# One pipeline of 24 chunks for the third feed-forward, with x in three bf16 parts, and a reordered first stage

## What is computed

```python
x = x + tanh(g_xattn[0]) * L0_xattn(ctx, norm(x))     # similarity graph, top 76 of each row
x = x + tanh(g_ffn[0])   * L0_ffn(norm(x))            # mixture of 16 experts, 6 chosen, and a shared one
x = x + tanh(g_xattn[1]) * L1_xattn(norm(x), ctx)     # latent attention, 16 heads
x = x + tanh(g_ffn[1])   * L1_ffn(norm(x))            # the one called "ternary" below
x = x + tanh(g_xattn[2]) * L2_xattn(norm(x), ctx, ctx)
x = x + tanh(g_ffn[2])   * L2_ffn(norm(x))
x = x + tanh(g_xattn[3]) * L3_xattn(norm(x), ctx)
x = x + tanh(g_ffn[3])   * L3_ffn(norm(x))

def quantize(w):                       # L1_ffn: weights become -1, 0 or 1
    return clip(round(w / (mean(abs(w)) + 1e-8)), -1, 1)
def L1_ffn(x, w1, w2, w3):             # w1, w2: 704 x 256, w3: 256 x 704
    x1, x2 = x @ quantize(w1).T, x @ quantize(w2).T
    return (sigmoid(x1) * x2) @ quantize(w3).T
```

## Time and profile before

| | us |
|---|---|
| median of 3 runs | 875.55 (875.4 to 877.6) |
| the profiled execution | 877.72, of it a span of 875.6 |

### The profile page before, as it was taken

One profiled execution on the slowest core, in us unless ns is written; L12 is line 12 of the kernel. 1 busy time (PEld: TensorE's weight loads), 2 busy tenths in 40 slices (PEclk: granted clock), 3 DMA queues, 4 the chain that ended last, 5 costly groups with the idle time before them and its releaser, 6 DMA issues.

```text
span 875.6 us, 13499 instructions
## 1 busy us (share of the span) xinstructions
PE 808.7 (92%) x4982; PEld 622.1 (71%) x4982; DVE 507.1 (58%) x1189; ACT 355.4 (41%) x1172; POOL 139.6 (16%) x146
## 2 busy tenths in 40 slices
PE   6799999999999999899997899998999999999973
PEld 3688888888888887677675567885667666666742
DVE  4677657657765534455567642325777664674742
ACT  2211111111111111667664661115887775675730
POOL 0000120000000000000019700001343233232001
PEclk9999999999999999999999999997999999999985
DMA  8970200000011002300000000000000000000000
GB/s 281 375 174 3 82 1 1 1 1 1 1 60 40 0 1 80 104 1 1 1 1 1 1 1 1 1 0 0 2 1 2 1 1 1 1 2 13 5 23 12
DMA packets 16175, 28.02 MB, mean 32 GB/s; under 512 B 3648, under 2 KB 11824, under 8 KB 15856
## 3 DMA queue, kind: packets, MB, share of 16 engines
q1 hardware_dynamic: 16112, 27.19, 9.7%
HBM read 26.13 MB, written 1.05 MB: 31 GB/s over the span
## 4 chain that ended last, share of the span: by engine, by line
PE 80%; DVE 8%; ACT 7%; issue 2%; POOL 1%; DMA 0%; SPq 0%; ACTq 0%; DVEq 0%; POOLq 0%
PE PS L1478 20%; PE PS L1502 10%; PE PS L1707 5%; PE PS L1731 5%; PE PS L1682 5%; PE PS L1567 3%; PE PS L1757 3%; ACT arena L734 3%; PE PS L1672 3%; ACT arena L816 2%; PE PS L1583 2%; DVE arena L1150 2%; PE PS L1611 2%; PE PS L1599 2%; PE PS L1626 2%
## 5 line engine op out<-in xcount | busy, mean ns | idle before, releaser
L656 ACT ACTIVATE arena<-PS 128x256 f32<-128x256 f32 (+3 forms) x192 | 102.1, 559 | 97.9 <-PE PS L1567 39.1
L816 ACT ACTIVATE arena<-PS,W_d 128x256 f32<-128x256 f32 (+1 forms) x256 | 110.6, 449 | 8.7 <-DVE W_d L1216 4.4
L524 POOL TENSOR_TENSOR RS<-MV,eps 128x2 f32<-128x2 f32 x32 | 6.2, 195 | 652.9 <-DVE MV L932 635.8
L1478 PE MATMUL PS<-XT,W_g 128*128 128x256 f32 (+1 forms) x400 | 98.0, 388 | 0.0
L1478 PE MATMUL PS<-XT,W_u 128*128 128x256 f32 (+1 forms) x400 | 95.2, 380 | 0.0
L1502 PE MATMUL PS<-W_d,mlp_tmp 128*128 128x256 f32 (+1 forms) x400 | 94.1, 379 | 0.0
L698 ACT ACTIVATE tanh_g<-PS 128x512 f32<-128x512 f32 x48 | 28.7, 597 | 156.7 <-PE PS L1478 156.7
L1093 DVE TENSOR_TENSOR mlp_tmp<-mlp_tmp,PS 128x512 f32<-128x512 f32 (+1 forms) x52 | 34.7, 667 | 86.3 <-PE PS L1489 86.1
L1478 PEld LDWEIGHTS PS<-XT,W_u 128*128 128x128 f32 (+1 forms) x400 | 76.0, 190 | 11.0
L1478 PEld LDWEIGHTS PS<-XT,W_g 128*128 128x128 f32 (+1 forms) x400 | 74.6, 192 | 10.9 <-issue 1.2
L1502 PEld LDWEIGHTS PS<-W_d,mlp_tmp 128*128 128x128 f32 (+1 forms) x400 | 72.2, 190 | 8.7
(11 more groups left out here) (209 smaller groups left out, 1376.2 us busy)
## 6 DMA issues: line engine op xcount, KB each, us to landing
W_d<-in_w_d SPq DMA_DIRECT2D x1, 3072.0 KB, 10.6
arena<-in_wq SPq DMA_DIRECT2D x4, 512.0 KB, 6.1
arena<-in_wo1T SPq DMA_DIRECT2D x4, 512.0 KB, 7.8
W_g<-in_w_g SPq DMA_DIRECT2D x2, 1024.0 KB, 9.4
W_u<-in_w_u SPq DMA_DIRECT2D x2, 1024.0 KB, 11.3
arena<-in_wkq1T SPq DMA_DIRECT2D x4, 384.0 KB, 6.8
mlp_w<-in_w SPq DMA_DIRECT2D x1, 1408.0 KB, 6.0
W_g<-in_w_g SPq DMA_DIRECT2D x1, 1120.0 KB, 12.2
```

What stands on the lines that cost most here:

```text
L656: last = act.activation(dst, src, ACT.Copy)
L816: last = act.activation(PL[:, n % 2, k * S:k * S + w], PS[:, bank + x, i * S:i * S + w], ACT.Exp, bias=NML[:, n % 2, k:k + 1], accum_out=D ...
L1478: last = mm(PS[0:m, k, e * S:(e + 1) * S], w[:, d, f0:f0 + m], XT[p][:, d, :], start=d == 0, stop=d == 1)
```

## The change

It has seven parts.

1. Ternary becomes one list of 24 chunks g = 6b + k across the batches. PE runs `up1(g)` and `down1(g - 2)`; chunks rotate through banks 2, 3 and 4, the sum through 5 and 6. The transposes of the next x come at k = 2.
2. The signs of w1 and w2 are written in bf16 (`w12b`), and the normalised x is split into three bf16 parts (`XB`) whose sum is x: ACT copies the high part out of PSUM (`high_part`), POOL makes the other two (`parts_of`: subtract, copy, subtract, 512 columns each). `up1` is then 12 bf16 products in place of 4 in fp32. w3 and the hidden rows stay in fp32.
3. `up1(0)` and `up1(1)` stand among the last latent items; `late_scores(0)` stands ahead of `up1(23)`, `late_scores(1)` ahead of `down1(23)`. ACT writes the first queries straight from PSUM, and `late_exponents(0)` stands ahead of the tanh of chunk 23.
4. First stage: projections of one batch each instead of two; the similarity of batch 0 is formed after the first of them. All four steps of fold 0 stand ahead of `graph_turn(0)`, `fold(1, 0)` behind it and `fold(1, 3)` behind the first `turn`. The ten steps left run in batch 0 of the experts, two for each pass c = 3 to 7. On DVE the graph's `graph_norm(0)` moves from behind the mask to between rounds 2 and 3. SP issues fold group 1 earlier, and slices 1 and 2 of the expert weights behind waits for fold steps.
5. Latent start: `stats(1)` and the first normalisation move from between the first items into passes 11 and 12 of the experts' last batch; the first keys use bank 7 instead of 6.
6. Late: PE's `job_turn` moves from ahead of `late_turned` to the end of the item; ACT's `job_turned` moves behind its `late_turned`, and its `job_mixed` ahead of `late_exponents`.
7. Two additions of a bias and one normalisation at the start of late move from DVE to POOL.

```diff
+def ternary_fills():
+    order = []
+    for g in range(CHUNKS):
+        order.append((2 + g % 3, "up", g // CH1, g % CH1))
+        if g >= 2 and (g - 2) % CH1 == 0:
+            b = (g - 2) // CH1
+            order += [(5 + b % 2, "y", b, 0), (7, "turn", b, 0)]
+    return order
...
+START_FOLDS = [(0, 0), (0, 1), (0, 2), (0, 3), (1, 0), (1, 3)]
+LATER_FOLDS = [(1, 1), (1, 2), (2, 0), (2, 3), (2, 1), (2, 2), (3, 0), (3, 3), (3, 1), (3, 2)]
...
@@ gpsimd
-                pool.tensor_tensor(wf, wf, less[0:parts, 0:n], ALU.subtract).then_inc(ternary_ready, 1)
+                signs = w12b[:, 2 * k:2 * k + 2, :].rearrange("p a b -> p (a b)") if k < 2 else wf
+                pool.tensor_tensor(signs, wf, less[0:parts, 0:n], ALU.subtract).then_inc(ternary_ready, 1)
...
+            def parts_of(b):
+
+                bank, value = fill_at("ternary", "turn", b - 1) if b else fill_at("latent", "turn", NB - 1)
+                pool.wait_ge(drained[bank], value)
+                x, (high, mid, low) = XT[b % 2][:, :, :].rearrange("p c s -> p (c s)"), [XB[b % 2][:, k, :] for k in range(3)]
+                pool.tensor_tensor(rest, x, high, ALU.subtract).then_inc(part_split, 1)
+                pool.wait_ge(part_split, 2 * b + 1)
+                pool.tensor_copy(mid, rest).then_inc(part_split, 1)
+                pool.wait_ge(part_split, 2 * b + 2)
+                pool.tensor_tensor(low, rest, mid, ALU.subtract).then_inc(parts_ready, 1)
+                pool.wait_ge(parts_ready, b + 1)
+
+            parts_of(0)
+            for b in range(NB):
+                rstd(next_no("ternary", b))
+                if b + 1 < NB:
+                    parts_of(b + 1)
...
@@ scalar
+            def high_part(b, bank, value):
+
+                act.wait_ge(filled[bank], value)
+                act.activation(XB[b % 2][:, 0, :], PS[:, bank, :], ACT.Copy)
...
+            for g in range(1, CHUNKS):
+                b, k = g // CH1, g % CH1
+                hidden_tanh(g)
+                if k == 2 and b + 1 < NB:
+                    bank, value = fill_at("ternary", "turn", b)
+                    high_part(b + 1, bank, value)
+                    xt_out(value, (b + 1) % 2, bank)
+                elif k == 2:
+                    first_queries()
+                if g == CHUNKS - 2:
+                    late_exponents(0)
...
@@ scalar, late
-                if p == 5 and r:
-                    job_turned(r)
                 if p == 7 and r:
                     job_exp(r)
                 if n < ITEMS:
                     late_turned(n)
+                if p == 1 and r > 1:
+                    job_mixed(r - 1)
+                if p == 5 and r:
+                    job_turned(r)
...
@@ vector
+            for g in range(CHUNKS):
+                b, k = g // CH1, g % CH1
+                hidden_rows(g)
+                if k == 0:
+                    stats((b + 1) % NB)
+                if k == 1:
+                    ternary_next(b)
+                    if b:
+                        output("ternary", b - 1, CA[:, 2:3])
+                    else:
+                        output("latent", NB - 1, TG[:, 1:2])
...
+                if g == CHUNKS - 2:
+                    late_maximum(0)
             late_maximum(1)
+            output("ternary", NB - 1, CA[:, 2:3])
...
@@ tensor
+            def up1(g):
...
+                if k == 0:
+                    pe.wait_ge(parts_ready, b + 1)
+                bank = begin("ternary", "up", b, k)
+                for w in range(2):
+                    for c in range(2):
+                        for part in range(3):
+                            last = mm(PS[0:m, bank, w * S:(w + 1) * S], w12b[:, 2 * w + c, k * P:k * P + m],
+                                      XB[b % 2][:, part, c * S:(c + 1) * S], start=c == 0 and part == 0,
+                                      stop=c == 1 and part == 2)
+                last.then_inc(filled[bank], 1)
...
+            for b in range(2):
+                projected(b)
+                similarity(b)
+            projected(2)
+            fold(0, 0)
+            similarity(2)
+            projected(3)
+            fold(0, 1)
+            similarity(3)
+            fold(0, 2)
+            fold(0, 3)
+            pe.wait_ge(first_loaded, 16 * N_FIRST)
             graph_turn(0)
-            fold(0, 3)
+            fold(1, 0)
             turn(1, fill_at("moe", "turn", -1)[1] - 1)
+            fold(1, 3)
...
+            for g in range(2, CHUNKS):
+                b, k = g // CH1, g % CH1
+                if g == CHUNKS - 1:
+                    late_scores(0)
+                    down1(g - 3)
+                up1(g)
+                if g < CHUNKS - 2:
+                    down1(g - 2)
+                if k == 2:
+                    turn(next_no("ternary", b), fill_at("ternary", "turn", b)[1] - 1)
+            down1(CHUNKS - 3)
+            down1(CHUNKS - 2)
+            late_second_banks = fill_at("ternary", "up", NB - 1, CH1 - 2)
+            pe.wait_ge(drained[late_second_banks[0]], late_second_banks[1])
             late_scores(1)
+            down1(CHUNKS - 1)
```

More of the change, by code:

```diff
@@ L95, in biases_before @@
 def biases_before(what, r):
-    order = []
+    order = [("late", 0), ("late", 1)]
     for n in range(ROUNDS + 1):
@@ L184, in late_fills, with later_folds, fold_phase, graph_phase @@
     return order
+START_FOLDS = [(0, 0), (0, 1), (0, 2), (0, 3), (1, 0), (1, 3)]
+LATER_FOLDS = [(1, 1), (1, 2), (2, 0), (2, 3), (2, 1), (2, 2), (3, 0), (3, 3), (3, 1), (3, 2)]
+def later_folds(c):
+    m = 2 * (c - FOLD_AT)
+    return LATER_FOLDS[m:m + 2] if m >= 0 else []
+def fold_phase(n, k):
+    return "begin" if (n, k) in START_FOLDS else "moe"
+def graph_phase(b):
+    return "moe" if b else "begin"
 def moe_fills():
-    order = [("fold", 0, k) for k in range(3)] + [("graph", 0, 0), ("fold", 0, 3), ("turn", -1, 0)]
+    order = [("turn", -1, 0)]
     for b in range(NB):
@@ L192, in moe_fills @@
         if b + 1 < NB:
-            order += [("fold", b + 1, k) for k in range(4)] + [("graph", b + 1, 0)]
+            order += [("fold", n, k) for n, k in (LATER_FOLDS if b == 0 else ())] + [("graph", b + 1, 0)]
         else:
@@ L197, in moe_fills @@
     return [("moe",) + key for key in order]
+CHUNKS = NB * CH1
+def ternary_fills():
[6 more added lines that the diff above has]
+    return order
 def all_fills():
     banks = {k: ["start"] for k in range(8)}
+    for m, (n, k) in enumerate(START_FOLDS):
+        banks[7 - m % 2].append(("begin", "fold", n, k))
+    banks[5].append(("begin", "graph", 0, 0))
     banks[7] += moe_fills()
     for phase in PHASES:
-        if phase in ("latent", "late"):
-            for bank, what, b, k in latent_fills() if phase == "latent" else late_fills():
+        if phase != "moe":
+            for bank, what, b, k in {"latent": latent_fills, "ternary": ternary_fills, "late": late_fills}[phase]():
                 banks[bank].append((phase, what, b, k))
@@ L363, in build @@
         NML, DENL = cut(P, 2, 4), cut(P, 2, 2 * NH)
+        w12b = half(cut, P, 4, H1)
+        XB = [half(cut, P, 3, 2 * S) for _ in range(2)]
         cut = areas(W_g[:, :, :].rearrange("p a b -> p (a b)"), 0)
@@ L616, in _ @@
                     kind, of = job(r)
-                    normalise("job", r, of, XN, fill_at("late", *(("job_turn", r - 1) if r > 1 else ("turn", 1))))
+                    normalise("job", r, of, XN, fill_at("late", "job_turn", r - 1) if r > 1 else fill_at("ternary", "turn", NB - 1))
                     if kind == "lora":
@@ L1015, in _ @@
             stats(0)
-            graph_round(0, rounds)
+            graph_round(0, 1)
+            graph_round(0, 2)
+            graph_norm(0)
+            for r in range(3, rounds + 1):
+                graph_round(0, r)
             graph_mask(0)
-            graph_norm(0)
             graph_add(0)
@@ L1510, in _ @@
                     up(c)
+                    steps = later_folds(c) if b == 0 else []
+                    if steps:
+                        fold(*steps[0])
                     if c == 1:
@@ L1629, in latent_output, with down1 @@
                     last.then_inc(filled[bank], 1)
+            def up1(g):
+                b, k = g // CH1, g % CH1
+                m = min(P, H1 - k * P)
+                if g == 0:
+                    pe.wait_ge(ternary_ready, 12)
+                if k == 0:
[7 more added lines that the diff above has]
+                                      stop=c == 1 and part == 2)
+                last.then_inc(filled[bank], 1)
+            def down1(g):
+                b, k = g // CH1, g % CH1
+                m = min(P, H1 - k * P)
+                at_, value = fill_at("ternary", "up", b, k)
+                pe.wait_ge(drained[at_], value)
+                bank, _ = fill_at("ternary", "y", b)
+                if k == 0:
+                    begin("ternary", "y", b)
+                for i in range(2):
```

(6 more changed lines are left out.)

324 lines of the change are left out of this document (146 added, 178 removed).

## The result

| | before | after |
|---|---|---|
| median, us | 875.57 (875.4 to 877.6, 4 runs) | 838.98 (836.46 to 840.87, 4 runs) |
| the profiled execution, us | 877.72, span 875.6 | 840.87, span 838.7 |
| ratio of the times | | 0.9575, 95% interval 0.9546 to 0.9605 |

The change makes the kernel 36.6 us faster. The forecast was 840.7, with 34.9 us gained.

What follows compares the result with a forecast made beforehand. The prediction took PE to bound the kernel, with 80% of the chain of waits. Its terms, -12.1 - 9.1 - 4.5 - 1.2 - 8.0 = -34.9 us, took the median from 875.55 to 840.7 us, range 831 to 854.

Steps and rivals of the forecast that it cites:

- bf16 products: Ternary: `up` takes 1.32 us a chunk instead of 1.73; with seams and starting idle, -12.1 us, bounds -9 to -13.3.
- D: Ternary: weight loads not hidden behind the bf16 products, 28.2 us more, 868.9 us; chance 0.03.
- F: Ternary: bf16 products adding up in one place of a bank don't overlap, 75 us more, 916; chance 0.02.
- The parts: Ternary: POOL's operations for the bf16 parts take 1.3 to 1.4 us each, hidden with 1 us to spare.
- rival B: Ternary: POOL is late with the parts for each batch, 6.6 us of stall in all, 847.3 us; chance 0.14.
- Seam: From ternary's last product to item 4's scores: 21.9 us becomes 12.8, -9.1 us, bounds -3.7 to -9.9.
- Latent's start: Start of latent: first transposes at 355.7 instead of 360.19, -4.5 us, some 1.8 of it clock; bounds -2.9 to -4.9.
- First stage: Up to the experts' end: router 1.2 us later, two steps of 1.5 and 1.0 leave the experts; -1.2 us, bounds +1 to -3.
- Late: Late: PE's waits for transposes and queries of bank 7 go, -8.0 us, bounds -3 to -10.
- Rival E: Late: its waits only change place and the term is 0, 848.7 us; chance 0.05.
- The sum: Whole kernel: the five terms add to -34.9 us, giving a median of 840.7 us.

Runs made afterwards that it cites:

- the run with the scores behind: Kernel after with late's first scores, maxima and exponents moved back behind ternary's last product: 848.86 us.
- the repeated one: The kernel after measured once more with no edit: 839.76 us.
- the two with the signs later: Kernel after with POOL starting the signs of w1, w2 and w3 only behind latent's last normalisation, measured twice: 835.53 and 837.04 us.

## Why the prediction was right

**bf16 products: right in mechanism and size.** 0.110 was forecast and 0.109 measured; undone, 10.1 us come back. The loads of 98 ns are hidden, with 12 such products in a row: rivals D and F are out. The term is -11.3 instead of -12.1; I took half of the seams between batches away, and that smaller saving is where the rest most likely lies, which no run tests. The text was wrong that the change triples the loads of `up`: a chunk had 8 fp32 loads of 190 ns, hidden too, and has 12 of 98, so 1.5 us of loads became 1.2.

```profile
L1682 PEld LDWEIGHTS PS<-XT,mlp_w x192: 133/190/190, 527.8 to 591.6; 128*128 128x128 f32 x160, 128*64 128x64 f32 x32
```

The rule in the Trainium skill ("TensorE: Matmul & The Clock Gate", Part 3, The mechanism), that a load overlaps a running product only where their row groups differ, isn't borne out as it stands: both use all 128 rows here, and the measurement decides. The same section also lets a load run ahead when it goes to a background weight buffer; by that the rows would agree, and no run here tells whether it is so.

**The parts: rival B was priced from the wrong neighbour.** I took 1.3 to 1.4 us for each POOL operation, and 1 us of slack. The subtractions take 1.16 and the cast 0.61; the chain is done at 532.46 and PE asks for it at 534.86, 2.4 us later. The forecast stood since both values lie under the cover, but the slack was sized too small, and so the chance given to B came out high.

**Seam: right, -9.3 for -9.1.** The maxima and exponents lie under the last chunks, 0.44 us of idle is left where I put 0.8, and the clock stays up. That the clock followed from the idle time ahead, and not from the kind of work, was the step that mattered, and the run with the scores behind shows it: 7.9 us come back with the wait. The other 1.4 are the idle time ahead of the first scores and what no edit isolates.

**Latent's start: right, -4.5,** with 1.7 us of clock for the 1.8 in the text. The rest of latent, which I left at nothing, lost 1.1 in this profile and in the repeated one, and nothing in the third (160.5 us, 160.6 in the kernel before). Over 452 to 470 us, behind PE's wait of 3.62, the granted clock is 0.81 in the first two and 0.91 in the third, so the loss most likely comes with the clock of an execution and not with the change.

**First stage: half of it.** `graph_turn(0)` came at 34.29 and not at 33.7, and so the router at 43.03 and not at 42.4. The first two groups of the experts' products, 16 in all, took 6.5 us in place of 5.7 in the kernel before (42.87 to 48.57). From there to the experts' end 3.25 us were gained, 2.5 of them forecast: 1.9 + 0.8 - 3.25 is the -0.55. By the second of these groups, which takes 3.0 us to the next start (48.31 to 51.27) and 2.15 in the kernel before, with 1.73 at full and 3.46 at half speed, I estimate that full speed began at 50.8 us, and at 47.3 in the kernel before. The step that failed is that I priced the clock by the fold steps alone and took the experts' start as unchanged. The term isn't a fixed number: in three profiles of the kernel after the experts' last product ends at 343.09, 342.98 and 341.69, so it was -0.55, -0.7 and -1.95, within the bounds that stood beside it. The view of stretches gives a granted clock of 1.00 while these products take twice their time: the trace holds no record of the clock ahead of the same 50.8 and 47.3 us, and the view counts such time as full. There only the durations tell.

**Late: mis-sized, -12.3 for -8.0.** Idle time of PE between the same instructions fell from 13.9 to 5.0 us, so 8.9. The waits of the earlier trace rows gave 8.2 of it (8.5 less the 0.5 left for XN, and 0.2 besides), and the one for WT, which I had not listed, 1.4; a wait of 0.8 for L1946 is new. I had taken half a microsecond off for later exponents. What I left out is the clock behind a wait: in the kernel before, 8 products behind a wait of 1.37 us ran 1.3 us longer than in the kernel after, and the transposes behind them 0.4. The PE timeline of the kernel before:

```profile
790.91 3.31 PE L1773 MATMUL PS<-XT,W_u 128*128 128x256 f32 x8 [1.37 <-ACT WT L656]
794.01 1.20 PE L1731 MATMUL PS<-ident,arena 128*128 128x128 f32 x6
```

The kernel after has none of the four waits behind which this happens. The remaining 1.7 of the 12.3 (0.65 in the last chain) I haven't traced. Rival E is out: with part 6 undone the waits return and the time rises by 11.7.

**The sum: right, in part by luck.** Late gave 4.3 us more than its term, seam 0.2 more, and the other stages 2.5 less, so the errors cancelled to 2.0. The experiments bear the sum out, less closely than their medians make it look: 10.1, 9.1, 11.7 and about 6 are 37, against 36.6 for the whole, but over their own stages the four edits cost 10.4, 7.9, 11.7 and 4.5, so 34.5. The 0.55 of the first stage, the 1.0 of idle at the seam and the 0.65 of the last chain, less the 1.1 that latent lost, make it 35.6 of the 36.9 between the two profiles; 1.3 us have no experiment. I see no part that gives back what another gains; part 7 and the order of chunks across batches were not tested by themselves.

## What to carry to other kernels

Where one engine bounds every stage, a sum of its instructions by start-to-start times and of its idle times with their releasers gives the effect of a large change within a few microseconds. Add to an idle time of TensorE what may run at the lower clock behind it: at four waits of 1.4 to 1.9 us one group of products lost 1.3 to 1.7 us in each kernel that had them, and a wait of 3.3 us was followed by 14 us at half speed. A gain under some 2 us can't be told here from where in the execution the clock rises, so compare several profiles over the stage that was edited, from one instruction to another, rather than two medians.

## What the runs showed of the hardware

- A cast of 512 columns from fp32 to bf16 on GpSimd takes 0.61 us, half of a subtraction of 512 (1.16), and the subtraction that writes bf16 takes no longer than the one that writes fp32 in three batches of four (1.16; 2.01 us for the one that falls into latent).
- Four groups of eight products stand behind waits of 1.90, 1.36, 1.36 and 1.37 us. In each profile one of the four ran at half speed (3.3 to 3.7 us in place of 2.0), and another one each time: the fourth in the kernel before, the third with part 6 undone, the first with `job_mixed` alone undone. Eight products behind a wait of 0.94 us in the last chain took 1.97 us in seven profiles (the kernel before, the three of the kernel after, the two with the signs later, latent's start undone) and 3.6 to 3.75 in the seven others. So the length of a wait doesn't say whether the clock falls behind it. The Trainium skill ("TensorE: Matmul & The Clock Gate", Part 1, What's actually happening) states that how many products of a kernel run at the lower clock differs from run to run; the 16 products at the experts' start agree, with 6.5, 6.4 and 5.1 us in the three profiles of the kernel after.
- While GpSimd makes the signs, a normalisation of twice 256 columns on VectorE takes 7.23 us in place of 0.72, and a scaling of 1024 columns 3.2 to 4.1 in place of 1.23. Moving GpSimd's work moves a part of the loss to what VectorE does then: 12.2 us of it became 7.6, and 10.8 us of TensorE's waits in that stretch 8.8.
